# A gated attention block with a mixture of experts: routed tokens sorted into tiles, or two dense experts and a list of block-expert pairs

## What is computed

```python
x = x + tanh(g_xattn[0]) * attention(k=ctx_1024, v=ctx_1024, q=layernorm(x))   # one head, per block
n = layernorm(x)
shared = (silu(n @ shared_w1) * (n @ shared_w2)) @ shared_w3       # 128 -> 512 -> 128
scores = sigmoid(n @ router_w)                                      # 16 experts
_, top_idx = top_k(scores + expert_bias, 2)                         # two experts a token
gates = scores at top_idx, 0 elsewhere
routed = sum_e (silu(n @ w1[e]) * (n @ w2[e])) @ w3[e] * gates[:, e]  # 128 -> 128 -> 128
out = x + tanh(g_ffn[0]) * (shared + routed)
```

## Time and profile before

| | us |
|---|---|
| median of 3 runs | 98.94 |
| the 3 runs | 98.51, 98.94, 100.27 |
| span of the profiled execution, first to last instruction | 112.6 |
| PE busy in it | 81.5 |
| DVE, ACT, POOL busy in it | 41.3, 37.7, 48.7 |

### The profile page before, as it was taken

One profiled execution on the slowest core, in us unless ns is written; L12 is line 12 of the kernel. 1 busy time (PEld: TensorE's weight loads), 2 busy tenths in 40 slices (PEclk: granted clock), 3 DMA queues, 4 the chain that ended last, 5 costly groups with the idle time before them and its releaser, 6 DMA issues.

```text
span 112.6 us, 1632 instructions
## 1 busy us (share of the span) xinstructions
PE 81.5 (72%) x437; PEld 65.4 (58%) x437; DVE 41.3 (37%) x180; ACT 37.7 (33%) x102; POOL 48.7 (43%) x63
## 2 busy tenths in 40 slices
PE   4889999979999999970022999149694629399910
PEld 4768749959996556640012998139593529245900
DVE  0096008883823483000204335132272134122680
ACT  1326239682809742001003334013352123006700
POOL 4049960054000677777730036627357645730200
PEclk9999999997559999999555559976999975559998
DMA  2992009999993018453684658867741153212406
GB/s 42 286 333 113 0 4 265 147 144 174 158 148 48 23 45 255 129 128 129 128 223 88 184 170 214 262 184 210 199 160 50 47 174 89 60 41 73 122 10 177
DMA packets 19311, 15.31 MB, mean 136 GB/s; under 512 B 1424, under 2 KB 18448, under 8 KB 19296
## 3 DMA queue, kind: packets, MB, share of 16 engines
q1 hardware_dynamic: 16208, 11.57, 46.9%
q0 software_dynamic: 1184, 2.44, 6.3%
q10 hardware_dynamic: 1904, 1.14, 4.5%
HBM read 9.14 MB, written 6.00 MB: 134 GB/s over the span
## 4 chain that ended last, share of the span: by engine, by line
PE 54%; another core or an unknown queue 13%; issue 13%; DMA 5%; DVE 5%; ACT 4%; ACTq 2%; DVEq 0%
PE bank L1054 7%; PE bank L1062 7%; PE bank L1055 6%; DMA ctx_sb<-in_ctx_dram 5%; PE bank L863 5%; PE bank L878 4%; PE bank L1012 3%; PE bank L1021 3%; PE bank L1043 3%; PE bank L902 3%; PE bank L1013 3%; PE bank L963 2%; DVE hid L738 2%; PE bank L908 2%
## 5 line engine op out<-in xcount | busy, mean ns | idle before, releaser
L472 POOL DMA_INDIRECT placed_y<-tile_y,tile_place x21 | 20.1, 957 | 23.1 <-DVE tile_place L806 13.5
L461 POOL DMA_INDIRECT sorted_x<-x2n,slot x16 | 15.5, 972 | 14.7 <-DMA sorted_x<-tile_x 10.1
L1054 PE MATMUL bank<-tile_xT,tile_w 128*128 128x128 f32 x44 | 11.3, 347 | 7.4 <-issue 4.8
L1062 PE MATMUL bank<-tile_w,tile_hid 128*128 128x128 f32 x44 | 10.3, 328 | 7.0 <-issue 3.8
L1054 PEld LDWEIGHTS bank<-tile_xT,tile_w 128*128 128x128 f32 x44 | 8.7, 246 | 8.6 <-issue 8.6
L573 ACT ACTIVATE silu_t<-bank 128x512 f32<-128x512 f32 x8 | 4.8, 597 | 26.0 <-remote 15.4
L606 ACT ACTIVATE tile_silu<-bank 128x128 f32<-128x128 f32 x22 | 6.1, 277 | 19.8 <-PE bank L1055 10.8
L1062 PEld LDWEIGHTS bank<-tile_w,tile_hid 128*128 128x128 f32 x44 | 8.0, 230 | 8.0 <-issue 8.0
L813 DVE TENSOR_TENSOR tile_hid<-tile_silu,bank 128x128 f32<-128x128 f32 x22 | 6.3, 286 | 17.2 <-ACT tile_silu L606 10.0
L1043 PE MATMUL bank<-ident,tile_x 128*128 128x128 f32 x24 | 6.2, 351 | 8.3 <-issue 8.3
L738 DVE TENSOR_TENSOR hid<-silu_t,bank 128x512 f32<-128x512 f32 x8 | 5.5, 686 | 17.3 <-issue 11.1
(11 more groups left out here) (132 smaller groups left out, 121.6 us busy)
## 6 DMA issues: line engine op xcount, KB each, us to landing
tile_w<-in_routed_w_dram SPq DMA_DIRECT2D x22, 192.0 KB, 2.4
sorted_x<-tile_x SPq DMA_DIRECT2D x1, 2967.0 KB, 21.2
tile_x<-sorted_x SPq DMA_DIRECT2D x8, 129.0 KB, 2.3
shared_sb<-in_shared_w_dram SPq DMA_DIRECT2D x1, 768.0 KB, 7.6
tile_x<-sorted_x ACTq DMA_DIRECT2D x4, 129.0 KB
x_sb<-in_x_dram SPq DMA_DIRECT2D x2, 256.0 KB, 4.9
picked_y<-placed_y SPq DMA_DIRECT2D x2, 256.0 KB, 3.3
picked_y<-placed_y SPq DMA_DIRECT2D x4, 128.0 KB, 2.4
```

The lines of the kernel that those rows point to most:

```text
L461: pool.indirect_dma_start(sorted_x[:, :], bass.IndirectOffsetOnAxis(slot[:, k * B + b:k * B + b + 1], 0), x2n[:, k, b, :], None).then_inc( ...
L472: pool.indirect_dma_start(placed_y[:, :], bass.IndirectOffsetOnAxis(tile_place[:, j:j + 1], 0), tile_y[:, j, :], None).then_inc(y_placed[j ...
L1054: nc.tensor.matmul(dst[:, 0:P], tile_w[:, j % WEIGHT_RING, 0:P], xt, start=True, stop=True)
L1062: nc.tensor.matmul(bank[j % 2][:, 0:D], tile_hid[:, j % 3, :], tile_w[:, j % WEIGHT_RING, 2 * P:3 * P], start=True, stop=True)\
```

## The change

Sorting, scatters, gathers, the DRAM scratch and the branches per tile go. Instead:

- All work is in four groups of two blocks (256 columns), attention too. `keys` multiplies the context by one fused matrix (`kq`) that carries the query weights and the scale; the scores are then xn times that. The order on every engine is written out by hand, and groups overlap.
- Each block's router logits come from the normalised, transposed x, two blocks at a time; ACT takes tanh in place of the sigmoid. DVE chooses per group (`choose`).
- One count of tokens per block and expert (two bf16 products) gives the two most used experts (`pick_dense`) and the list of eight block-expert pairs (`pick_places`). The two experts run over all tokens, each in four chunks of 256 columns; each pair runs over its whole block, two pairs a chunk. The gate of a token that did not choose the expert is 0.
- SP reads two and then eight expert numbers into registers and starts ten weight loads. PE reads eight block offsets, and DVE sixteen (gate and block) for the sums.
- One stream of 28 chunks runs through TensorE: 16 shared, 4 of the first expert, 4 of pairs, 4 of the second expert. `up` of chunk k is issued two chunks ahead of `down`, over three PSUM banks.
- POOL takes two of the four second normalisations, the sum of x and the bias, the power of -0.5 and the gates.
- If more than eight pairs are used, every engine takes a branch behind the end that runs all sixteen experts over all tokens.

The core of the diff:

```diff
-            sp.wait_ge(padding_ready, 1)
-            sp.dma_start(sorted_x.rearrange("(j p) d -> p j d", p=P), tile_x[:, :, :]).then_inc(rows_zeroed, 16)
...
+            sp.wait_ge(dense_expert_ready, 1)
+            _, dense = nc.values_load_multi_w_load_instructions(
+                dense_expert[0:1, :], engines=[mybir.EngineType.SP], min_val=0, max_val=E - 1,
+                skip_runtime_bounds_check_because="four bits")
+            for i in range(DENSE):
+                load_expert(i, dense[i])
+            sp.wait_ge(places_ready, 3)
+            _, placed = nc.values_load_multi_w_load_instructions(
+                place_expert[0:1, :], engines=[mybir.EngineType.SP], min_val=0, max_val=E - 1,
+                skip_runtime_bounds_check_because="four bits")
+            for j in range(PLACES):
+                load_expert(DENSE + j, placed[j])
+
+            for g in range(G):
+                sp.wait_ge(final_ready, g + 1)
+                sp.dma_start(o_dram[:, twos(g), :], final[:, twos(g), :]).then_inc(stored, 16)
...
-                    pool.indirect_dma_start(sorted_x[:, :], bass.IndirectOffsetOnAxis(slot[:, k * B + b:k * B + b + 1], 0),
-                                            x2n[:, k, b, :], None).then_inc(rows_scattered[k], 16)
...
+            copy_ctx(0, bank[0])
+            act.wait_ge(kq_done, 1)
+            nc.scalar.copy(kq[:, :], bank[2][:, 0:D]).then_inc(kq_ready, 1)
+            act.wait_ge(rows_loaded, 16)
+            nc.scalar.activation(tanh_g[:, :], gains, ACT.Tanh).then_inc(tanh_ready, 1)
+            copy_ctx(1, bank[3])
+            copy_x(0, bank[4])
...
+            def pick_dense():
+                dve.wait_ge(counts_done, 1)
+                step(nc.vector.reduce_sum(total[:, :], counts.rearrange("p (b e) -> p e b", b=B), AX))
+                step(nc.vector.scalar_tensor_tensor(expert_key[:, :], total[:, :], float(E), expert_back[:, :], ALU.mult, ALU.add))
+                step(nc.vector.max(dense_key[:, :], expert_key[:, :]))
+                step(nc.vector.tensor_copy(dense_bits[:, :], dense_key[:, 0:DENSE]))
...
+            def pick_places():
...
+                step(nc.vector.max(place_key[:, :], pair_key[:, :, :].rearrange("p b e -> p (b e)")))
...
+            def share(k):
+                dve.wait_ge(silu_ready, k + 1)
+                if k >= 3:
+                    dve.wait_ge(down_done, k - 2)
+                nc.vector.tensor_tensor(hid[:, k % 3, :], silu_t[:, k % 3, :], bank[UP_BANK[k % 3]][:, 256:512], ALU.mult)\
+                    .then_inc(hid_ready, 1)
...
+            moments_x2(3)
+            share(0)
+            choose(0)
+            share(1)
+            choose(1)
+            share(2)
...
+            share(8)
+            sum_shared(0)
+            share(9)
+            pick_dense()
+            share(10)
+            pick_places()
+            share(11)
+            count_pairs()
...
+            for g in range(G):
+                add_first(g)
+                share(FIRST + 2 + g)
+
+            _, gate_at = nc.values_load_multi_w_load_instructions(
+                place_gate[0:1, :], engines=[mybir.EngineType.DVE], min_val=0, max_val=B * E,
...
+            _, block_at = nc.values_load_multi_w_load_instructions(
+                place_block[0:1, :], engines=[mybir.EngineType.DVE], min_val=0, max_val=B * P,
...
+            for q in range(PLACES // 2):
+                add_places(q)
+                share(PLACED + 2 + q)
...
+            pairs = dve.value_load(pair_count[0:1, 0:1], min_val=0, max_val=B * E)
+            with dve.If(pairs > PLACES):
...
+            def up(k, w1, w2, g):
+                if k >= 3:
+                    pe.wait_ge(hid_ready, k - 2)
+                dst = bank[UP_BANK[k % 3]]
+                nc.tensor.matmul(dst[:, 0:256], w1, x2nT[:, twos(g), :], start=True, stop=True)
+                nc.tensor.matmul(dst[:, 256:512], w2, x2nT[:, twos(g), :], start=True, stop=True).then_inc(up_done, 1)
...
+            for k in range(10, SHARED):
+                share_up(k)
+                share_down(k - 2)
+            dense_up(0, 0)
+            share_down(SHARED - 2)
+            dense_up(0, 1)
+            share_down(SHARED - 1)
+            dense_up(0, 2)
+            pe.wait_ge(places_ready, 3)
+            pe.wait_ge(count_ready, 1)
+            dense_down(0, 0)
+            dense_up(0, 3)
+            dense_down(0, 1)
+            _, block_at = nc.values_load_multi_w_load_instructions(
+                place_block[0:1, :], engines=[mybir.EngineType.PE], min_val=0, max_val=B * P,
+                skip_runtime_bounds_check_because="a block of nine")
...
+                    xt = x2nT_flat[:, bass.ds(block_at[j], S)]
+                    nc.tensor.matmul(dst[:, i * P:(i + 1) * P], tile_w[:, DENSE + j, 0:P], xt, start=True, stop=True)
```

More of the change, by code:

```diff
@@ new lines, in _ @@
+            copy_x2(3, bank[5])
+            silu(6)
+            silu(7)
+            squash(3, bank[2])
+            for k in range(8, CHUNKS):
+                silu(k)
+            act.wait_ge(count_ready, 1)
+            pairs = act.value_load(pair_count[0:1, 0:1], min_val=0, max_val=B * E)
+            with act.If(pairs > PLACES):
+                for k in range(2 * E):
+                    act.wait_ge(rest_up_done, k + 1)
+                    if k >= 1:
+                        act.wait_ge(rest_hid_ready, k)
+                    nc.scalar.activation(rest_silu[:, :], bank[7][:, :], ACT.Silu).then_inc(rest_silu_ready, 1)
@@ L1104, in _ @@
-            for k in range(SHARED_EARLY, 2 * HJ):
-                share_up(k)
-            for k in range(HJ, 2 * HJ):
-                pe.wait_ge(hid_ready, 2 * HJ - 1)
-                share_down(k)
+            values(0, bank[3])
+            turn_ctx(3, bank[1])
+            keys(2, bank[5])
+            pe.wait_ge(bias_ready, 1)
+            score(1, bank[6])
+            values(1, bank[0])
+            turn_probs(0, bank[7])
+            pe.wait_ge(vo_ready, 1)
+            turn_x(2, bank[3])
@@ new lines, in _ @@
+            keys(3, bank[2])
+            attend(0, bank[4])
+            score(2, bank[1])
+            turn_probs(1, bank[5])
+            turn_x(3, bank[7])
+            pe.wait_ge(vo_ready, 2)
+            values(2, bank[0])
+            attend(1, bank[6])
+            score(3, bank[3])
+            turn_probs(2, bank[2])
+            values(3, bank[1])
+            pe.wait_ge(x2_ready, 2)
+            attend(2, bank[4])
+            turn_x2(0, bank[5])
+            turn_probs(3, bank[3])
+            pe.wait_ge(shared_loaded, 16)
@@ new lines, in place_down @@
+            def place_down(q):
+                k = PLACED + q
+                pe.wait_ge(hid_ready, k + 1)
+                pe.wait_ge(acc_ready, 2 + 2 * (G + q - 2))
+                dst = bank[Y_BANK[k % 3]]
+                for i in range(2):
+                    last = nc.tensor.matmul(dst[:, i * D:(i + 1) * D], hid[:, k % 3, i * P:(i + 1) * P], tile_w[:, DENSE + 2 * q + i, 2 * P:3 * P],
+                                            start=True, stop=True)
+                last.then_inc(down_done, 1)
```

1351 lines of the change are left out of this document (621 added, 730 removed).

## The result

| | kernel before | kernel after |
|---|---|---|
| median of the timed runs, same chip, us | 99.60 (98.51 to 100.29, 4 runs) | 68.72 (68.47 to 69.11, 4 runs) |
| ratio, 95% interval | | 0.693 (0.688 to 0.699) |
| span of the profiled execution, us | 112.6 | 66.4 |

The forecast was 68 us. In two later series of runs the kernel after took 68.83 and 69.17 us, the kernel before 96.18 and 98.64.

The account below looks back on a forecast made before the run. The prediction took POOL's one-by-one scatters, with sorted rows arriving late, to bound the kernel. Its terms 25.3 + 36.2 + 4.9 + 3.5 gave a 69.9 us span, less 2 for timed runs: 68 us, range 60 to 80.

Parts of the forecast that it names:

- A: Start to the first `share_down`: `attend(0)` at 16.2 us, then DVE's list sets the pace; 25.3 us, bounds 22.8 and 28.
- B: The stream of 28 chunks: TensorE works without a break at the full clock; 36.2 us.
- C: What breaks the stream: routing on DVE, register reads of TensorE and DVE, addresses from registers; 4.9 us.
- D: The end: `add_second(3)` 0.7 us, then the store 2.8; 3.5 us.
- rival 2: Timed runs shrink against the span as before, part A at its lower bound, reads 1 us: about 60 us, 12%.
- (1): Between `share(8)` and `share(13)`: routing work on DVE delays the stream by 1.0 us, bounds 0 and 2.
- (2): In front of `place_up(0)`: TensorE's eight register reads cost 2.0 us, between about 0.6 and 4.4.
- (3): Beside the pairs' chunks: DVE's sixteen register reads take 3.5 us, 2.3 of it free; 1.2 us, bounds 0 and 6.5.
- (4): In the pairs' products: addresses from registers for 16 products cost 0.7 us, bounds 0 and 2.
- 1 fell: Rival for the stream: TensorE stays at the lower clock, or register reads are dear; about 79 us, 20%.
- 3 was not taken: Rival at the end: the branch for more than eight pairs is taken, adding 130 us; about 200 us, 3%.
- 4 fell: Rival in the stream's second half: routing answers so late that TensorE waits for weights; about 78 us, 1%.

Follow-up runs that it names:

- experiment 9: Kernel before with each of the sixteen row scatters issued twice, the second time to a list nobody reads: 117.2 us against 99.8.
- experiment 3: Kernel after without the eight warm-up products on TensorE ahead of the first load: 69.29 us against 68.72 to 69.17.
- Experiments 5 and 7: Two separate edits of the kernel after: POOL's first bias sum ahead of the last group's normalisation, 68.07 us; POOL's two normalisations moved to DVE, 67.98 us.
- experiment 1: Kernel after with the first up product of each of the 16 shared chunks done twice: 75.34 us, 6.2 to 6.6 more.
- Experiment 2: Kernel after with expert numbers, block offsets and gate positions written in as constants, no register reads for them, weight loads early: 68.20 us.
- experiment 7: Kernel after with POOL's two normalisations of x (groups 2 and 3) moved to DVE: 67.98 us, 0.85 less.
- experiments 5 to 8: Kernel after with POOL's sum earlier (68.07 us), last hids ahead of DVE's sums (68.45), normalisations on DVE (67.98), the last two together (68.48; repeated 68.22 against 69.17).

## Why the prediction was right, and where it was not

The time was right within about 1% and each big term within 0.6 us but one, yet 68 came out of two errors that cancelled:

| | forecast | measured (profile after) |
|---|---|---|
| A, start to first `share_down` | 25.3 | 25.0 |
| B, the stream | 36.2 | 36.3 (25.03 to 62.3, where the last result is out, less C) |
| C, what breaks it | 4.9 | 1.0 (0.22 + 0.8) |
| D, the end | 3.5 | 4.1 (62.3 to 66.4) |
| span | 69.9 | 66.4 |
| from the span to the timed runs | -2 | +2.1 (68.47 for the execution with the profile) |

**The rows behind the scatters.** Right, and shown by experiment 9: the earlier trace rows name the queue that set the time before. Part A's remark that the groups buy little stands untested.

Some sums of the prediction don't come out as printed: 42 passes of 0.21 us are 8.8, not 9.0; A's lower bound is 9.3 + 4.6 + 9.1 = 23.0, not 22.8; rival 2 works out at 58 (66.4 x 0.88), not 60; and all bounds of A and C together reach from 61 to 81, not from 62 to 75. None moves the forecast by more than 0.2 us.

**A was right by compensation.** The parameters let tanh start at 6.62 us, not 8.09, and the copy of woT at 8.35. The clock was not half way to 16.6 but up by 6.89 (experiment 3: the warm-up products, which I overlooked). So `attend(0)` was done near 14.0 us, not 16.2. But then the residual waited 1.39 us for POOL's sum, which stood behind two pairs of normalisations of 1.6 us each: a queue on POOL that I had not costed (these are the first normalisations of groups 2 and 3, which the section on the change leaves out). It started at 15.30, forecast 16.2. From there to the end of the first hid 9.25 us passed, forecast 9.1, but it was not DVE's list that set them. The chain leaves DVE at 17.21 us for ACT, reaches the first `up` at 21.08, and from there TensorE works without a break to the first `share_down`. ACT's softmax, copies and table load on that way stood at nothing in the sum, although the chain of the kernel before has the same load:

```profile
23.56 1.28 ACT L545
```

No experiment moved it, so its price is open. Experiments 5 and 7 show that POOL's list was worth 0.35 us in the traces, 0.76 and 0.85 by the medians.

**B was right.** A chunk takes 0.43 + 0.43 + 0.45, as priced from the earlier trace rows; experiment 1 shows that TensorE paces it, and the full clock is in every stretch from 25 to 62 us.

**C is the term that was mis-sized.** (1) Routing took 1.0 in the forecast and nothing in the trace: from 37.45 to 41.40 us DVE was busy 3.64 us and TensorE without a break. (2) TensorE's reads: 2.0 against 0. The price of one read was near the low end of my bounds (0.78 us), but I had put it on the array's path. The queue reads while the array works on products that were queued before; it has to be later than these to cost anything, and it was 1.2 us earlier. (3) DVE's sixteen: 1.47 us in two instructions, of which 0.22 reached TensorE; forecast 1.2. (4) Addresses: 0.7 against nothing visible. Experiment 2 bounds (2) to (4) together, and more with them, at 1 us by the times; its trace puts them at 0.22. What I had not listed is the 0.8 us ahead of the last `down`, where a sum stands before the hid in DVE's list.

The price that the prediction weighed from a page does not hold here: the Trainium skill, "Runtime: NRT & Kernel Launch", section "Instruction fetch mechanics", has some 200 ns a register in bulk, and speaks there of register loads that the runtime inserts. Here the kernel reads tiles that DVE wrote, and TensorE's eight took 777 ns and DVE's sixteen 1466, about 0.1 us each; the measurement decides.

**The weights** were covered, as said: first issue at 39.46 us, 2.8 to land, so 42.3, and `dense_up(0, 0)` at 44.4. The cover left is 2.1 us, forecast 2.7.

**The shared port.** A pair of normalisations on DVE took 0.59 us with POOL idle (experiment 7, 17.73 us), and 0.59 and 0.60 beside a power or a small operation of POOL (6.95 and 7.87 us in the kernel after). So a power did not hold them, and the 4.1 us that the prediction weighed didn't come. Beside POOL's sums of x and the bias a pair took 0.67 and 0.71 in the kernel after, 1.04 and 0.99 in experiment 7. A hold like the lock in the Trainium skill, "SBUF — State Buffer", section "SBUF: two separate sides", fits these last rows and not the ones beside a power; it wasn't tested by itself.

**D** was 0.6 short. SP's reading of the count of pairs and its branch (63.4 to 64.0) are not the reason, since SP waits 1.7 us more for the transfer behind them. The stores took up to 2.8 us to land (2.3 in the median), those of the kernel before 2.0; why is open.

**Span and timed runs: the step failed in its sign.** I took 2 us off, since the span of the earlier trace rows was 13.7 above the median. In all timed runs here whose span is known, of either kernel, the time stands 1.9 to 3.0 us above the span of the same execution; for the kernel before these spans are 93.1 to 98.4. So the profile of 112.6 us was of one unusual execution, not of a general relation. In it SP's smallest instructions took up to 704 ns; with even more scatters, in experiment 9, at most 28. So the scatters' traffic is not what stretched them, as I had argued; what did stays open. The -2 rested on that argument alone.

**The rivals.** 1 fell: no low clock in the stream, reads hidden. 2 fell with the step above. 3 was not taken; its price is 144 us, forecast 130 (4.28 a chunk for 4.06, and 7 us of start and end). 4 fell.

**The marks.** POOL without a DMA, the first hid near 25 us (24.14), passes of 0.215 and 0.112 us: as said. No gap before `place_up(0)`: wrong. DVE waits for TensorE's `down` (3.3 us) more than for silu (1.7): the order of these two was wrong, the direction right.

## What to carry to other kernels

A register read costs what is late behind it, not its own length: issue it behind a few us of queued products, eight values in one instruction, and it vanishes, as here; on an engine whose results TensorE awaits next, a part of it shows. Before a profiled span is used as the base of a sum, put it beside the timed runs: where it is 14% longer, take durations from it, but neither its gaps nor its relation to the timed runs. When one engine fills the stream, what is left to gain lies at the two ends of it, in the order of the other engines' lists: here 0.35 us at the front by moving one line. Where such a gain is smaller than the scatter of the times, measure it as a distance between two events inside the traces, so that the landing of the loads falls out.

## What was not expected of the hardware

- A read of several registers is priced by the instruction more than by the value: two values 0.67 us and eight 0.54 on SP, eight 0.78 on TensorE, 0.60 and 0.87 on DVE.
- Eight warm-up products before the first real work brought the full clock by 7.9 us in ten of eleven profiles, and not before some 10.5 in the other, of the same kernel.
- The first hid starts between 24.14 and 25.12 us in three profiles of the same kernel. In the second one (24.84) TensorE waits 0.87 us for a piece of the context where the first waits 0.19; in the third the clock is late. That scatter is as large as the gains of experiments 5 to 8, so medians of six runs don't settle these; the distances in the table do.
- POOL's normalisation of 128 x 128 took 0.80 us, DVE's 0.30.
